# Mixture of a graph layer by seven products of halves, with the edge sums alone behind it

## What is computed

```
xn = layernorm(x)
gnn = segment_sum(norm[:, None] * (xn @ W.T + b)[col], row)      # edges and own node
q', k' = relu(split(xn @ Wq.T + bq) @ P.T) / 8, the same with Wk  # 16 heads of 64
mix = (q' @ (k'.T @ v)) @ Wo.T + bo
x1 = x + gnn + mix
out = x1 + sum over 8 experts of weight * ((silu(n @ Wg) * (n @ Wu)) @ Wd),  n = layernorm(x1)
```

## Time and profile before

| | |
|---|---|
| median of 3 runs | 1088.25 us (1088.06 to 1088.41) |
| the profiled execution | 1088.11 us |
| its span, from the first to the last instruction | 1086.2 us |
| TensorE busy | 1075.5 us, 99% |
| VectorE, ScalarE, GpSimd busy | 441.6, 269.9, 323.0 us |
| DMA | 162.36 MB, mean 149 GB/s |

### The profile page before, as it was taken

How to read it: one execution, slowest core, us unless ns; L and a number is a source line. 1 busy time by engine, 2 the same in 40 slices (tenths; PEclk the granted TensorE clock), 3 DMA queues, 4 the chain that set the end, 5 groups by cost and what they waited for, 6 DMA issues and landing times.

```text
span 1086.2 us, 15078 instructions
## 1 busy us (share of the span) xinstructions
PE 1075.5 (99%) x5587; PEld 893.3 (82%) x5587; DVE 441.6 (41%) x1061; ACT 269.9 (25%) x413; POOL 323.0 (30%) x223
## 2 busy tenths in 40 slices
PE   8999999999999999999999999999999999999998
PEld 7887778887878888888878888887788888888887
DVE  6944666676641111322212123344235112314684
ACT  5320211112233345311111112434213112202221
POOL 4000011122132347400035444434208744500151
PEclk9999999999999999999999999999999999999999
DMA  7313011122244487604179987876045646205912
GB/s 269 97 30 108 13 35 54 61 70 72 70 128 127 159 296 247 209 1 155 39 196 327 307 243 205 235 218 186 1 160 189 213 179 214 66 24 221 378 66 110
DMA packets 148731, 162.36 MB, mean 149 GB/s; under 512 B 8150, under 2 KB 116018, under 8 KB 145330
## 3 DMA queue, kind: packets, MB, share of 16 engines
q1 hardware_dynamic: 148082, 159.55, 45.5%
q10 hardware_dynamic: 576, 1.84, 0.4%
HBM read 114.91 MB, written 46.45 MB: 149 GB/s over the span
## 4 chain that ended last, share of the span: by engine, by line
PE 95%; DVE 3%; issue 1%; ACT 1%; DMA 0%; ACTq 0%; DVEq 0%
PE ps L1773 10%; PE ps L1774 9%; PE ps L1775 9%; PE ps L2073 7%; PE ps L2074 7%; PE ps L2075 7%; PE ps L2014 4%; PE ps L2008 4%; PE ps L1988 3%; PE ps L1989 3%; PE ps L1939 3%; PE ps L1990 3%; PE ps L1940 3%; PE ps L1941 3%; PE ps L2131 3%; PE ps L2132 3%
## 5 line engine op out<-in xcount | busy, mean ns | idle before, releaser
L1773 PE MATMUL ps<-w_hi,xnH 128*128 128x512 f32 x464 | 184.7, 398 | 0.0
L1775 PE MATMUL ps<-w_hi,xnL 128*128 128x512 f32 x464 | 180.9, 390 | 0.0
L1774 PE MATMUL ps<-w_lo,xnH 128*128 128x512 f32 x464 | 180.8, 390 | 0.0
L827 POOL TENSOR_TENSOR acc<-acc,cw 128x320 f32<-128x320 f32 x40 | 35.7, 892 | 252.6 <-ACT cw L1028 251.4
L1773 PEld LDWEIGHTS ps<-w_hi,xnH 128*128 128x128 f32 x464 | 87.1, 188 | 18.8
L1775 PEld LDWEIGHTS ps<-w_hi,xnL 128*128 128x128 f32 x464 | 87.1, 188 | 18.6
L1774 PEld LDWEIGHTS ps<-w_lo,xnH 128*128 128x128 f32 x464 | 87.2, 188 | 17.0
L1675 DVE TENSOR_TENSOR prd<-ps,wB 128x512 f32<-128x512 f32 (+1 forms) x24 | 14.2, 592 | 142.1 <-PE ps L2075 101.2
L1939 PE MATMUL ps<-xnH,w_hi 128*128 128x512 f32 (+1 forms) x192 | 68.1, 355 | 0.0
L2073 PE MATMUL ps<-x2H,guH 128*128 128x512 f32 (+1 forms) x192 | 67.7, 352 | 0.4 <-ACT wT L1232 0.4
L2074 PE MATMUL ps<-x2L,guH 128*128 128x512 f32 (+1 forms) x192 | 67.6, 352 | 0.0
(11 more groups left out here) (421 smaller groups left out, 2127.0 us busy)
## 6 DMA issues: line engine op xcount, KB each, us to landing
cR<-c_d SPq DMA_DIRECT2D x20, 640.0 KB, 5.2
foldin<-in SPq DMA_DIRECT2D x32, 256.0 KB, 2.8
guR<-in SPq DMA_DIRECT2D x16, 512.0 KB, 5.7
w_raw<-in SPq DMA_DIRECT2D x14, 512.0 KB, 6.4
c_d<-cw SPq DMA_DIRECT2D x40, 160.0 KB
wdq<-in SPq DMA_DIRECT2D x6, 1024.0 KB, 7.3
qs0H<-qT_d SPq DMA_DIRECT2D x10, 512.0 KB, 5.2
qs0L<-qT_d SPq DMA_DIRECT2D x10, 512.0 KB, 6.5
```

Source lines behind the costliest of these rows:

```text
L1773: pe.matmul(target, xnH[:, kc, cols], wH[w][:, kc, :], start=(kc == 0), stop=False)
L1774: pe.matmul(target, xnH[:, kc, cols], wL[w][:, kc, :], start=False, stop=False)
L1775: mm = pe.matmul(target, xnL[:, kc, cols], wH[w][:, kc, :], start=False, stop=(kc == KC - 1))
```

## The change

The 20 `mixture(i)` of 24 matmuls are replaced by the scheme of the down projection, `seven_products(0, q, r)`: 7 products of 5 groups of 12 matmuls, all ahead of the edge sums. Its parts are shared now by both stages (`s` = 0 mixture, `s` = 1 down).

- The q stage stores q' unsplit (half of the bytes); m_low also copies the block of M unsplit (`mR`), and SP stores it (`mr_d`).
- In the h stage, in four rounds k, SP loads four blocks of M (`load_mix_blocks`), POOL makes four sums of blocks and later the low parts, ACT rounds (`mix_high`, one after each of h jobs 2 to 17), and SP stores high and low part (`store_mix_block`) in `mt_d`. One buffer `mixH` takes all high parts, so each rounding waits for the store of the one before.
- SP loads the panels of products 0 and 1 after block 11, ahead of the loads of round 3. The q tiles come in 10 loads `load_q(t)`: tiles 0 to 2 between the stores of blocks 12 to 15, tile 3 behind block 15's, tiles 4 to 9 behind that. The first token groups wait for tiles 0 to 4 (`in_q[0]`), DVE waits for tiles 5 to 9 (`in_q[1]`) ahead of its third.
- Results of the products, with x added, go to DRAM (`x1_d`) in half rows. In the sum stage, `load_half` and `load_rest` fetch them from there, instead of x.
- The sum stage has only `aggregate(i)` on TensorE. The counts have five buffers and are loaded two steps ahead. The orders on ACT and DVE change as shown; x2_transposes(t) comes one step later (behind the sums of tile t+2), x2_hi and x2_low three tiles behind.

The diff, cut to its core:

```diff
@@ SP, end of the h stage
+            for k in range(3):
+                load_mix_blocks(k)
+                for n in range(4 * k, 4 * k + 4):
+                    store_mix_block(n)
             sp.wait_ge(*made(("h", 0, NT - 1)))
-            for piece in range(4):
-                load_m(0, piece)
+            for q in range(2):
+                load_mix_panel(q)
+            load_mix_blocks(3)
+            for n in range(12, 16):
+                store_mix_block(n)
+                load_q(n - 12)
+            for t in range(4, NT):
+                load_q(t)
...
+            def load_mix_blocks(k):
+                if k:
+                    sp.wait_ge(wd_st[1], 64 * k)
+                for j, (h, g) in enumerate(((0, k), (1, k), (0, k + 4), (1, k + 4))):
+                    sp.dma_start(mixR[j][:], mr_d[h, :, g, :]).then_inc(in_d[0], 16)
...
+            def load_q(t):
+                sp.wait_ge(*made(("h", 1, t)))
+                cols = slice(t * P, (t + 1) * P)
+                for k in range(2):
+                    sp.dma_start(qR[k][:, :, cols], qT_d[4 * k:4 * k + 4, :, cols].rearrange("k q n -> q k n"))\
+                      .then_inc(in_q[t // HALF], 16)
@@ ACT, h stage
+            def mix_high(n):
+                act.wait_ge(wd_mix, 4 * (n // 4) + (1, 2, 4, 3)[n % 4])
+                if n:
+                    act.wait_ge(wd_lo, n)
+                    act.wait_ge(wd_st[0], 16 * n)
+                act.activation(mixH[:], mixR[MIX_MADE[n % 4][0]][:], ACT.Copy).then_inc(wd_hi, 1)
...
+                    if 3 <= NT * hf + t < 19:
+                        mix_high(NT * hf + t - 3)
+                    if hf and t == NT - 1:
+                        token_high(0, 0)
+                        token_high(0, 1)
                     h_high(hf, t)
@@ ACT, sum stage
             for i in range(2 * NT):
                 t = i - NT
-                if i + 1 < 2 * NT:
-                    count_high(i + 1)
-                if t == NT - 1:
+                if t >= 3:
+                    for h in range(2):
+                        x2_hi(t - 3, h)
+                if i + 2 < 2 * NT:
+                    count_high(i + 2)
+                if t >= 0:
                     ln2_sqrt(t)
-                if t >= 1:
-                    for h in range(2):
-                        x2_hi(t - 1, h)
-                if 0 <= t < NT - 1:
-                    ln2_sqrt(t)
-                if t >= 0:
                     ln2_out(t)
                 if t == NT - 2:
                     gu_high(0)
+            for t in (NT - 3, NT - 2):
+                for h in range(2):
+                    x2_hi(t, h)
@@ DVE, mixture and sum stage
+            dve.wait_ge(in_q[1], 32 * HALF)
+            seven_products(0)
...
             for i in range(2 * NT):
                 t = i - NT
+                if t >= 3:
+                    x2_low(t - 3)
                 add_sums(i)
-                if i + 1 < 2 * NT:
-                    add_mixture(i + 1)
-                if 1 <= t < NT - 1:
-                    x2_low(t - 1)
+                if i + 1 < NT:
+                    add_bias(i + 1)
                 sum_stats(i)
                 if t >= 0:
                     ln2(t)
-                if t == NT - 1:
-                    x2_low(t - 1)
-            x2_low(NT - 1)
+            for t in range(NT - 3, NT):
+                x2_low(t)
@@ TensorE
-            mixture(0)
+            for q in range(7):
+                for r in range(HALF):
+                    seven_products(0, q, r)
             for i in range(2 * NT):
-                if i + 1 < 2 * NT:
-                    mixture(i + 1)
                 aggregate(i)
-                if i >= NT + 1:
-                    x2_transposes(i - NT - 1)
+                if i >= NT + 2:
+                    x2_transposes(i - NT - 2)
+            x2_transposes(NT - 2)
```

More of the change, by code:

```diff
@@ new lines, in store_mixture, with load_c @@
+            def store_mixture(d):
+                hf, t = down_out(d)
+                sp.wait_ge(d_dr, d + 1)
+                sp.dma_start(by4(x1_d[t][:, hf * W:(hf + 1) * W]), room(0, d)).then_inc(mix_st, 16)
+            def load_c(i):
+                t, before = i % NT, C_BEFORE[i]
+                if before >= 0:
+                    sp.wait_ge(a_done, before + 1)
+                    sp.wait_ge(c_lo, before + 1)
+                sp.dma_start(cR[C_ROOM[i]][:], c_d[:, :, t * P:(t + 1) * P].rearrange("c q r -> q c r"))\
+                  .then_inc(in_c[i % 4], 16)
@@ new lines, in _ @@
+            load_mix_panel(2)
+            for d in range(HALF):
+                store_mixture(d)
+            load_mix_panel(3)
+            sp.wait_ge(mix_st, 16 * HALF)
+            load_rows(1)
+            for q in (4, 5):
+                sp.wait_ge(d_mm, HALF * (q - 1))
+                load_mix_panel(q)
+            sp.wait_ge(hx_lo, 4 * HALF)
+            load_rows(2)
+            for d in range(HALF, 2 * HALF):
+                store_mixture(d)
+            sp.wait_ge(d_mm, 5 * HALF)
@@ new lines, in add_earlier @@
+            def add_earlier(s, d):
+                g, r = d // HALF - 1, d % HALF
+                pool.wait_ge(*room_in(s, d))
+                pool.wait_ge(u_ok, 2 * HALF * s + (0, HALF, 0)[g] + r + 1)
+                earlier = u3(s, r) if g == 1 else u2[s][:, r]
+                pool.tensor_tensor(room(s, d), room(s, d), earlier, ALU.add).then_inc(o_sum, 1)
+            for d in range(HALF, 2 * NT):
+                add_earlier(0, d)
+            def add_bias(i):
+                t = i - NT
+                pool.wait_ge(in_bo, 32)
+                pool.wait_ge(in_rest[t % 4], 16 * (t // 4 + 1))
+                pool.tensor_tensor(xt[t % 4][:, W:D], xt[t % 4][:, W:D], bob[1][:], ALU.add).then_inc(x_in[1], 1)
@@ new lines, in third_sum, with fourth_sum, result @@
+            def third_sum(s, r):
+                dve.tensor_tensor(tokens(s, 0, r + HALF), tokens(s, 0, r), tokens(s, 0, r + HALF), ALU.subtract).then_inc(hs, 1)
+            def fourth_sum(s, r):
+                dve.tensor_tensor(tokens(s, 1, r), tokens(s, 1, r), hs2[s][:, r], ALU.subtract).then_inc(hs, 1)
+            def result(s, d, group):
+                if d < HALF:
+                    dve.wait_ge(*room_in(s, d))
+                else:
+                    dve.wait_ge(o_sum, 3 * HALF * s + d - HALF + 1)
+                dve.tensor_tensor(room(s, d), by4(down_bank(group, d % HALF)), room(s, d), ALU.add).then_inc(d_dr, 1)
@@ new lines, in seven_products @@
+            def seven_products(s):
+                for i in range(2, 7 * HALF + 3):
+                    if i < 7 * HALF:
+                        token_low(s, i)
+                    if i >= 3:
+                        product_out(s, i - 3)
+                    if 4 <= i < 4 + HALF:
+                        first_sums(s, i - 4)
+                    if 9 <= i < 9 + HALF:
+                        third_sum(s, i - 9)
+                    if 18 <= i < 18 + HALF:
+                        fourth_sum(s, i - 18)
@@ new lines, in seven_products @@
+            def seven_products(s, q, r):
+                i, target = q * HALF + r, down_bank(GROUP[q], r)
+                bank_is_free(s, q, r)
+                if r == 0 and s == 0:
+                    for part in range(2):
+                        pe.wait_ge(in_w[0][2 * (q % 2) + part], 48 + 16 * (q // 2 + 1))
+                elif r == 0 and q < 2:
+                    pe.wait_ge(wd_lo, 16 + 6 + q)
+                elif r == 0:
+                    pe.wait_ge(in_wd[min(q - 2, 2)], 32 if q < 4 else 96)
+                pe.wait_ge(hx_lo, 7 * HALF * s + i + 1)
+                opens = q not in (1, 4, 6)
+                panel_hi, panel_lo = seven_panel(s, q)
+                for k in range(4):
+                    hi, lo = hxH[s][i % 3][:, k, :], hxL[s][i % 3][:, k, :]
+                    high, low = panel_hi[:, k, :], panel_lo[:, k, :]
+                    pe.matmul(target, hi, high, start=(opens and k == 0), stop=False, skip_group_check=not opens)
+                    pe.matmul(target, hi, low, start=False, stop=False, skip_group_check=not opens)
+                    mm = pe.matmul(target, lo, high, start=False, stop=(k == 3), skip_group_check=not opens)
+                mm.then_inc(d_mm, 1)
```

580 lines of the change are left out of this document (287 added, 293 removed).

## The result

The changed kernel takes **1125.57 us** (median of 4 runs, 1124.96 to 1126.82) against 1088.15 for the kernel before on the same chip: a ratio of **1.0345, 95% interval 1.0327 to 1.0363**. That is 37.4 us slower, and 19 us more than the 1106.4 that were forecast. The span of its profiled execution is 1123.1 us.

The account below looks back on a forecast made before the run. TensorE, busy 1075.5 of 1086.2 us, was taken as the bound. Matmul savings, late start, sums, loop, way out and clock, chained as profile times, put the first expert at 783.5 against 765.2: 1088.11 + 18.3 = 1106.4 us; range 1091 to 1114.

Parts of the forecast that it names:

- What it saves: Mixture on TensorE: 420 matmuls instead of 480, 60 x 0.227 = 13.6 us saved; the products' work on other engines costs nothing.
- The start: Start of the products: late blocks and q tiles move group 2 from 554.5 to 568.4, costing 13.9 us (bounds 1 and 17).
- I take 4.6 and 3.3: Round 3 of the mixed blocks: waits in us of blocks 14 and 15 for the store before, giving 549.3.
- ACT and DVE add 1.6: Conversion of the first tokens: 1.6 us after q tiles 3 and 4 land at 557.7, so first product at 559.3.
- The wait of 3 to 4 us before the third group: Sign in the products: TensorE waits again before the third group, ending with a DVE wait on q.
- The first half of the sums: Edge sums up to add 12: thirteen at 4.54 us, plus 1 us for late counts and loads (bounds 0 and 6).
- The loop of 6.64 us: Sums' second half: ACT and DVE's closed loop holds TensorE to 6.64 us, not 5.32, a step: +9.2, and +1.9 for gu_high(0).
- The way out: From the last add to the first expert matmul: 14.5 us against 9.0, so +5.5.
- The clock: TensorE's clock falls after idling before the experts: +1.7 us (bounds 0 and 3.4); nothing at the products' start.
- The fourth: Rival on the sums: counts land 2 us later, some 1126, or the clock falls in the loop's gaps, 1134; 9%.

Follow-up runs that it names:

- the last run: Kernel with reordered start, counts' loads first and second LayerNorm one tile behind, plus later expert weight loads and swapped rooms for tokens 0 and 1: 1079.25 us (0.9918).
- e2: Changed kernel with two buffers for the high halves of the mixed blocks, so a rounding waits for the store before the last: 1120.7 us (1.0289).
- e1: Changed kernel with the panels of products 0 and 1 loaded behind round 2's loads, not ahead of round 3's: 1124.21 us (1.0333).
- e5: Changed kernel with q tiles 0 to 7 loaded right behind round 3's block loads, 8 and 9 behind the stores of blocks 12 and 13: 1127.06 us (1.0361).
- e6: Changed kernel with two high-half buffers, round 3's loads first, panels and q tiles reordered, and DVE's wait for tiles 5 to 9 later: 1111.74 us (1.0222).
- e7: Changed kernel with SyncE issuing the counts' load two steps ahead in front of the half-row store, not behind it: 1116.13 us (1.0265).
- e8: Changed kernel with POOL's subtraction for the counts' low parts cut to 32 columns of one chunk, those unused low parts left out: 1121.65 us (1.0303).
- e4: Changed kernel with the first half's bias added by POOL, as in the kernel before, instead of by DVE: 1123.22 us (1.0325).

## Why the prediction was wrong

The direction was right (slower, 82%), its size was not: 1125.6 lies above the range. Along its steps:

- **What it saves, 13.6 us: right**, and shown by the last run's busy time. The products took 2.72 us a group (576.8 to 666.5 for 33), as costed, and their ACT, DVE and POOL work stayed hidden.
- **The start: right mechanism, term mis-sized.** The cost was 22.3 us (554.5 to 576.8), not 13.9, and above the bound of 17. "Block 11 is rounded after h tile (1, 3), at 517.2": it was rounded at 520.6, since round 2 already hung on its own chain (loads landed at 507.0, POOL's sums and low part to 514.2, then the stores: 514.2, 517.5, 520.6) and not on the tiles of h; so the panels came at 523.1 instead of 519.5. The loads behind them landed at 539.85 instead of 534.8, 1.5 us of it in the queue. "I take 4.6 and 3.3": blocks 14 and 15 came 6.3 and 3.1 us apart, as a q tile's two loads stood in front of the store. q tiles 3 and 4, issued behind block 15 as written, took 7.6 us to land, not 6.3. And "ACT and DVE add 1.6": it was 2.6, since the product was released by the last bias of h behind both low parts, and not by `token_low` of tile 0. Together the first product came 9.8 us late. The wait of 3 to 4 us before the third group did not come: the first group took 4.9 us at the lower clock, and so tile 5 was there in time. 9.8 + 2.2 - 3.6 is the 8.4 us of the miss that lie here. Of this, two buffers alone gave 4.9 us (e2), the panels (e1) or the q tiles (e5) moved alone gave nothing, and all of it together gave 13.8 (e6); how the 13.8 divides stays open.
- **The first half of the sums: the step that was missing.** "I take 1 us for all of this, bounds 0 and 6" was said of late counts; up to add 12 the loss was 8.7 us, above that bound too and 7.7 more than taken. The prediction never cost `add_bias` on DVE, which the change moves there, nor asked what stands behind the late addition: SP's store, and behind that the counts' load. e7 removed it (9.4 us, with the second half's part) and leaves 0.8 us up to add 12; e8 took away only its first link (3.9), and so did e4 (2.4, within the noise).
- **The loop of 6.64 us: right**, 6.61 measured, and 8.50 with `gu_high(0)` where 8.54 was worked out. But the steps into adds 13, 17 and 18 took 7.93, 7.46 and 7.91, which makes 3.2 us beyond the forecast's sum. The prediction had seen that late counts would hold the square root there, and put all of them in its 1 us. e7 takes these three away by the place of the counts' load alone.
- **The way out: right.** 15.8 us with its clock, against 14.5 + 1.7.
- **The clock: right** where it was costed (0.78 at the way out), and nearly so at the start ("nothing"): the slow first group took 2.2 us more, but all except 0.6 of it fell into the time in which the third group's tokens were not ready. It fell at one more place, 0.91 from 700 to 720, behind a wait of 2.1 us.
- **The rivals.** The fourth comes nearest in time (1126), but not by its mechanism: counts held the square root in three steps of seven, not in all, and no clock fell within the loop's gaps. The sum of the misses, 8.4 + 7.7 + 3.2 - 0.4, is the 19 us.

The Trainium skill would have given the first link of the missing step. "SBUF — State Buffer", in the section SBUF: two separate sides, says that a VectorE operation with two SBUF inputs and a GpSimd operation that reads SBUF take turns by an exclusive lock for a whole instruction. The trace agrees: 3.2 us beside 2.9, 0.69 without, and an addition that reads one operand from PSUM stays at 0.74 us in the midst of the same subtraction (at 730.1). What the long addition then holds up, SP's store and the load behind it, is not in it. On 512-byte pieces, for which the prediction cited the Trainium skill ("DMA: Bandwidth & Descriptors", Specifications), the trace again differs from it: 284 GB/s at a share of 1.12 from 560 to 570 with q tiles alone, against the 262 and the 423 of the earlier trace rows.

## What to carry to other kernels

Where an engine issues its loads in order, ask of each load what stands in front of it and what that waits for; a prefetch behind a store of fresh results is no prefetch. Removing work from the bounding engine pays only when the loops that its work had hidden are shorter than what is left: here 13.6 us less of matmuls came out as 37 us more, and with another order of issues, a second buffer and other rooms as 8.9 us less. Before moving one link out of a loop, look for every engine that waits for it.

## What the runs showed of the hardware

- VectorE's addition of two SBUF operands of 128x512: 0.69 us alone, 3.2 beside a GpSimd subtraction of 2.94 us, and ended 0.6 us after it each time.
- SyncE's issue of a 256 KB load in 512-byte pieces takes about 0.5 us at its usual best (1.05 for two in the changed kernel), and 1.3 to 1.5 on average in a long row of loads (21.02 us for 16 in e5, 8.76 for 6 in e6, the longest single one 5.05): the issuing engine is held, not only the transfer.
- After waits of 19.5, 5.4 and 2.1 us the granted clock was 0.50, 0.78 (over 20 us) and 0.91 (over 20 us); ten matmuls behind a wait of 2.1 us took 4.10 us instead of 2.43. Behind a wait of 3.1 us (742.3) it stayed at 1.00, so the length of the wait alone does not decide it.
